# Weight segments in every second group of inputs, and the bias of q as a 129th column of the correlation

## What is computed

```python
q = layernorm(x) @ Wq + bq;  k = ctx @ Wq + bq;  v = k      # 16 columns each
corr = real(ifft(fft(q) * conj(fft(k)))).mean(batch, head)   # along the 128 positions
W, I = top_k(corr, 12);  W = softmax(W)
R = sum_j W[j] * roll(v, -I[j])
x = x + repeat(R) @ Wout + bout
x = x + fp4_linear(silu(fp4_linear(n, w_gate)) * fp4_linear(n, w_up), w_down)   # n = layernorm(x)
```

## Time and profile before

| | |
|---|---|
| Median of 3 runs | 572.26 us (572.17 to 574.67) |
| The profiled execution | 570.98 us, of which the span is 569.2 us |
| PE busy | 466.8 us (82%), 3454 instructions |
| DVE busy | 463.4 us (81%), 748 |
| ACT busy | 394.4 us (69%), 666 |
| POOL busy | 284.1 us (50%), 366 |
| DMA | 69.19 MB moved, mean 122 GB/s |

### The profile page before, as it was taken

The page is one execution under the profiler, slowest core; times in us unless marked ns, Lnnn a source line. Parts: engine busy times, 40 slices in busy tenths (PEclk is TensorE's granted clock), DMA queues, the critical chain, the costliest instruction groups (busy, mean ns, idle before and its releaser), DMA issues. The chain is left out here.

```text
span 569.2 us, 10045 instructions
## 1 busy us (share of the span) xinstructions
PE 466.8 (82%) x3454; PEld 307.0 (54%) x3454; DVE 463.4 (81%) x748; ACT 394.4 (69%) x666; POOL 284.1 (50%) x366
## 2 busy tenths in 40 slices
PE   5277995408799899998989999998999999999944
PEld 5266994303355555655556555565555655556633
DVE  2899657356889999989999999998999999997760
ACT  2378555456887778888887777888888777776530
POOL 3053530066556665565566666555556666622231
PEclk9699998757899999999999999999999999999977
DMA  9965930323246665555655576555655556445433
GB/s 276 306 220 157 293 119 15 87 57 76 51 84 119 128 118 113 107 123 120 124 117 106 126 117 129 108 109 129 120 117 116 112 126 109 95 89 107 79 78 78
DMA packets 165042, 69.19 MB, mean 122 GB/s; under 512 B 129152, under 2 KB 164736, under 8 KB 164992
## 3 DMA queue, kind: packets, MB, share of 16 engines
q1 hardware_dynamic: 164416, 68.03, 52.9%
q10 hardware_dynamic: 576, 0.53, 0.3%
HBM read 27.90 MB, written 9.18 MB: 65 GB/s over the span
## 5 line engine op out<-in xcount | busy, mean ns | idle before, releaser
L723 PE MATMUL ps<-guT_hi,a_xT 128*128 128x512 f16 (+1 forms) x384 | 140.6, 366 | 50.3 <-DMA a_xT<-ctx_sb 50.3
L428 POOL TENSOR_TENSOR ctx_sb<-h_c,sl 128x704 f16<-128x704 f16 x64 | 96.1, 1523 | 115.8 <-DVE ctx_sb L953 115.8
L733 PE MATMUL ps<-dT_hi,hqT 128*128 128x256 f16 x704 | 132.5, 277 | 11.9 <-DMA hqT<-ctx_sb 11.9
L724 PE MATMUL ps<-guT_lo,a_xT 128*128 128x512 f16 (+1 forms) x384 | 140.3, 365 | 0.0
L725 PE MATMUL ps<-guT_hi,a_xT 128*128 128x512 f16 (+1 forms) x384 | 140.0, 365 | 0.0
L723 PEld LDWEIGHTS ps<-guT_hi,a_xT 128*128 128x128 f16 x384 | 37.8, 98 | 98.6 <-DMA a_xT<-ctx_sb 40.4
L735 PE MATMUL ps<-dT_lo,hqT 128*128 128x256 f16 x384 | 89.6, 277 | 0.0
L482 ACT ACTIVATE h_c<-y_h 128x1408 bf16<-128x1408 bf16 (+3 forms) x40 | 49.2, 1230 | 55.2 <-DVE y_h L983 35.0
L733 PEld LDWEIGHTS ps<-dT_hi,hqT 128*128 128x128 f16 x704 | 70.0, 99 | 25.0 <-DMA hqT<-ctx_sb 12.7
L466 POOL TENSOR_TENSOR xs<-xs,w_raw 128x512 f32<-128x512 f32 x32 | 38.1, 1192 | 69.5 <-issue 49.1
L948 DVE SCALAR_TENSOR_TENSOR hb<-ps,h_in,w_raw 128x704 f32<-128x704 f32 x64 | 60.5, 945 | 2.6 <-PE ps L725 2.5
(11 more groups left out here) (140 smaller groups left out, 854.9 us busy)
## 6 DMA issues: line engine op xcount, KB each, us to landing
w_raw<-a_scratch SPq DMA_DIRECT2D x64, 128.5 KB, 2.7
xs<-in_x_dram SPq DMA_DIRECT2D x16, 512.0 KB, 5.7
ctx_sb<-in_ctx_dram SPq DMA_DIRECT2D x16, 512.0 KB, 4.5
out_dram<-a_xT SPq DMA_DIRECT2D x64, 128.0 KB, 2.0
hqT<-ctx_sb SPq DMA_TRANSPOSE x64, 3.7
w_raw<-in_L_ffn_w_down_dram SPq DMA_DIRECT2D x1, 704.0 KB, 5.2
w_raw<-in_L_ffn_w_gate_dram SPq DMA_DIRECT2D x1, 640.0 KB, 5.9
w_raw<-in_L_ffn_w_up_dram SPq DMA_DIRECT2D x1, 640.0 KB, 7.1
```

The lines of the kernel that those rows point to most:

```text
L428: pool.tensor_tensor(hq[:, j % 2, t, FF:2 * FF].rearrange("p (ih r) -> p ih r", ih=IH), h_c[:, :].bitcast(F16).rearrange("p (ih t r) -> p ...
L723: pe.matmul(dst, xt[:, c, :], guT[0][:, c, n0:n1], start=(c == 0), stop=False)
L724: pe.matmul(dst, xt[:, c, :], guT[1][:, c, n0:n1], start=False, stop=False)
L733: pe.matmul(dst, hqT[:, j % 4, c, :], dT_hi[:, c, :], start=(c == 0), stop=False)
```

## The change

The segments of w_gate and w_up are spread: a function `turn(i)` gives the segment whose turn comes in group `i`. With `W_FIRST = 0` segments 0 to 5 are begun in groups 0, 2, 4, 6, 8 and 10. `w_split` goes with `turn(i)`, `w_finish` with `turn(i - 1)`, `w_hi` and `w_lo` with `turn(i - 2)`; the order of the calls inside a group stays.

The product of k with bq is no longer issued. q and k of a group, which lay in one tile, lie in two; the one for q has a 129th column that holds bq and is written once, before the loop. The product of k and q takes 129 columns, and bank 7 holds the sum of the bias in its column 128. After the loop ScalarE takes this column into `g_bias` and adds it, as a bias per partition, in both copies of `g2`, in the function Identity where it was Copy.

```diff
--- before.py
+++ after.py
@@ -54,6 +54,7 @@
 SEGS = [(256 * c, 256 * min(2, GU_CH - c)) for c in range(0, GU_CH, 2)] + [(256 * GU_CH + FF * j, FF) for j in range(2)]
 WCOLS = 256 * GU_CH + 2 * FF
 N_GU = len(SEGS) - 2
+W_FIRST = 0
 NP = B // 2
 IH = BLK // 2
 RUN_H, RUN_X = 2 * NBH, 2 * NBX
@@ -133,9 +134,11 @@
         ident_out = sb("ident_out", [P, P])
         wq_x = sb("wq_x", [P, KC, SLOT])
         a_xT = sb("a_xT", [P, 2, 2 * QT, P])
-        qkT = sb("qkT", [P, 2, 2, P])
+        qT = sb("qT", [P, 2, P + 1])
+        kT = sb("kT", [P, 2, P])
         v_all = sb("v_all", [P, B * DH])
         g2 = sb("g2", [P, 2, P])
+        g_bias = sb("g_bias", [P, 1])
         dg = sb("dg", [P, P])
         corr = sb("corr", [P, 3, P + 4])
         top = sb("top", [P, 2, 8])
@@ -194,7 +197,7 @@
             "c_loaded0", "c_loaded1", "c_loaded2", "c_loaded3", "attn_loaded0", "attn_loaded1",
             "stored0", "stored1", "stored2", "stored3", "consts", "w_steps", "w_pool", "w_lo", "w_hi", "w_split", "root_set", "w_tr", "w_ev",
             "stats", "pool_a", "wq_sum", "r_ev", "wq_mid", "trx", "trc", "evx", "evc", "proj", "qk_ev", "v_tr", "v_ev",
-            "g_done", "g_ev", "g_io", "t_steps", "t_pe", "t_exp", "t_io", "a_io0", "a_io1", "a_io2", "a_io3", "m_sums",
+            "q_bias", "g_done", "g_col", "g_ev", "g_io", "t_steps", "t_pe", "t_exp", "t_io", "a_io0", "a_io1", "a_io2", "a_io3", "m_sums",
             "x1_done", "sq_done", "pool_st", "xn_ready", "x_max", "sc_steps", "sh_done", "s32", "sl", "x_split", "x4_steps",
             "h_steps", "h_split", "h4_steps", "loh", "o_done", "id_out",
             "hT0", "hT1", "hT2", "hT3", "xT0", "xT1", "gate_done", "gu_done", "sil_done", "d_done")}
@@ -227,6 +230,10 @@
         def scratch(w, g):
             o, n = SEGS[g]
             return w[:, FF * max(0, g - N_GU):FF * max(0, g - N_GU) + n]
+
+        def turn(i):
+            k = i - W_FIRST
+            return k // 2 if k >= 0 and k % 2 == 0 and k // 2 < N_GU else None
 
         def seg_at(g):
             return 7 + K_W * g + (7 if g >= N_GU else 0)
@@ -414,8 +421,8 @@
             for i in range(NQ):
                 if i + 2 < NQ:
                     rstd_a(i + 2)
-                if 0 <= i - 2 < N_GU:
-                    w_lo(i - 2)
+                if turn(i - 2) is not None:
+                    w_lo(turn(i - 2))
 
             largest(1)
 
@@ -515,13 +522,15 @@
                     evac_x(i, u)
                 if i % QT == 2 and i > QT:
                     keep_v(i // QT - 1)
-                if 0 <= i < N_GU:
-                    w_split(i)
-                if 0 <= i - 2 < N_GU:
-                    w_hi(i - 2)
+                if turn(i) is not None:
+                    w_split(turn(i))
+                if turn(i - 2) is not None:
+                    w_hi(turn(i - 2))
             act.wait_ge(s["g_done"], NQ)
-            act.activation(g2[:, 0, :], bank(7)[:, 0:P], ACT.Copy).then_inc(s["g_ev"], 1)
-            act.activation(g2[:, 1, :], bank(7)[:, 0:P], ACT.Copy).then_inc(s["g_ev"], 1)
+            act.activation(g_bias[:, :], bank(7)[:, P:P + 1], ACT.Copy).then_inc(s["g_col"], 1)
+            act.wait_ge(s["g_col"], 1)
+            for k in range(2):
+                act.activation(g2[:, k, :], bank(7)[:, 0:P], ACT.Identity, bias=g_bias[:, 0:1]).then_inc(s["g_ev"], 1)
 
             keep_v(NQ // QT - 1)
             evacuate_weights(act, range(EARLY))
@@ -633,11 +642,12 @@
 
             def correlate(i):
                 pe.wait_ge(s["qk_ev"], i + 1)
-                pe.matmul(bank(7)[:, 0:P], qkT[:, i % 2, 1, :], qkT[:, i % 2, 0, :], start=(i == 0), stop=False)
-                pe.matmul(bank(7)[:, 0:P], qkT[:, i % 2, 1, :], bq_col[:, :].broadcast_to([P, P]), start=False, stop=(i == NQ - 1)
+                if i == 0:
+                    pe.wait_ge(s["q_bias"], 1)
+                pe.matmul(bank(7)[:, 0:P + 1], kT[:, i % 2, :], qT[:, i % 2, :], start=(i == 0), stop=(i == NQ - 1)
                           ).then_inc(s["g_done"], 1)
                 need(pe, s["v_ev"], i // QT)
-                pe.transpose(bank(6)[:, P * (i % QT):P * (i % QT + 1)], qkT[:, i % 2, 1, :], ident[:, :]).then_inc(s["v_tr"], 1)
+                pe.transpose(bank(6)[:, P * (i % QT):P * (i % QT + 1)], kT[:, i % 2, :], ident[:, :]).then_inc(s["v_tr"], 1)
 
             for i in range(NQ):
                 for u in range(2):
@@ -823,10 +833,10 @@
                 need(dve, s["g_done"], i - 1)
                 need(dve, s["v_tr"], i - 1)
                 out = bank(4 + i % 2)
-                dve.tensor_scalar(qkT[:, i % 2, 1, :], out[:, P:2 * P], bq_col[:, 0:1], None, ALU.add)
-                dve.tensor_copy(qkT[:, i % 2, 0, :], out[:, 2 * P:3 * P]).then_inc(s["r_ev"], 1)
+                dve.tensor_scalar(kT[:, i % 2, :], out[:, P:2 * P], bq_col[:, 0:1], None, ALU.add)
+                dve.tensor_copy(qT[:, i % 2, 0:P], out[:, 2 * P:3 * P]).then_inc(s["r_ev"], 1)
                 dve.wait_ge(s["r_ev"], i + 1)
-                dve.tensor_tensor(qkT[:, i % 2, 0, :], out[:, 0:P], qkT[:, i % 2, 0, :], ALU.mult).then_inc(s["qk_ev"], 1)
+                dve.tensor_tensor(qT[:, i % 2, 0:P], out[:, 0:P], qT[:, i % 2, 0:P], ALU.mult).then_inc(s["qk_ev"], 1)
 
             def w_prepare(part):
                 cols = cols_of(part * N_GU)[0]
@@ -859,18 +869,21 @@
                 last = dve.scalar_tensor_tensor(out=wq_x[:, c, :], in0=bank(7)[:, 0:SLOT], scalar=-1.0 / D, in1=wq_sb[:, c, :],
                                                 op0=ALU.mult, op1=ALU.add)
             last.then_inc(s["wq_mid"], 1)
+            for k in range(2):
+                last = dve.tensor_copy(qT[:, k, P:P + 1], bq_col[:, :])
+            last.then_inc(s["q_bias"], 1)
             w_prepare(0)
             for i in range(NQ):
                 if i + 2 < NQ:
                     stats_a(i + 2)
                 if i >= 1:
                     evac_qk(i - 1)
-                if i == 0:
+                if i == W_FIRST:
                     w_scales(0)
-                if 0 <= i - 1 < N_GU:
-                    w_finish(i - 1)
-                if 0 <= i < N_GU:
-                    w_segment(i)
+                if turn(i - 1) is not None:
+                    w_finish(turn(i - 1))
+                if turn(i) is not None:
+                    w_segment(turn(i))
             evac_qk(NQ - 1)
             cs = s["c_steps"]
 
```

## The result

The changed kernel took 565.99 us (median of 4 runs, 564.98 to 567.59) against 572.24 (4 runs, 572.17 to 574.67) for the kernel before in the same job: ratio 0.989, 95% interval 0.9861 to 0.9918. That is 6.25 us less; the forecast was 7.0 less and 565.3. The profiled execution is the slowest of the four, 567.59 us, of which 565.8 is span.

What follows compares the result with a forecast made beforehand. VectorE's queue bounds the first part at 5.44 us a group, TensorE the second at 3.72. Summed chains bring p(15), the last project's end, from 88.75 to 81.78, 7.0 earlier: 572.26 - 7.0 = 565.3 us, range 562.0 to 568.9.

Steps and rivals of the forecast that it cites:

- The pace of the pairs: Correlation stage: during the segments two groups take 7.7 to 8.1 us, TensorE waiting for ScalarE before every second group's transposes.
- p(next odd) = E + 7.57: Chain over ScalarE: from E, evac_qk's start on VectorE, to p, project's end in the next odd group, 7.57 us.
- the last segment: End of the segments: it has half the columns, estimated at 0.9 us less in the chain over ScalarE.
- E(1): Start of VectorE's evac_qk in group 1: stays at 30.76 us, since GpSimd returns from its all-reduce only at 27.43.
- The meetings: VectorE's w_finish beside GpSimd's w_lo in each pair: w_finish takes 2.36 us, without a meeting 1.51.
- The power of rstd: Rival: GpSimd's pow blocks VectorE's w_finish, 3.14 us in two or three pairs; 566.9 us, chance 0.10.
- TensorE alone: Rival: ScalarE's late evacuations never reach TensorE, all groups take 3.50 us; 560.2 us, chance 0.10.
- the gain is not there: Rival: something else sets the first part's 5.44 us a group, only the removed product pays; 570.5 us, chance 0.05.
- the clock falls: Rival: stalls moved to every second group make TensorE's clock fall in the stage; slower, chance 0.05.
- Behind it the same times: After the correlation's hand-over: unedited code keeps its times; wrong if its length changes by more than 1 us.
- The table load of the upper end: ScalarE's Identity with bias at the copies of g: a table load, over 1 us, not expected, only in the upper bound.
- The product's 0.23 per group: TensorE in the correlation stage: without the second product an unhindered group falls from 3.72 to 3.49, say 3.50 us.

Runs made afterwards that it cites:

- e1: The changed kernel run again in another job, nothing edited: 565.56 us, ratio 0.9883 to the kernel before.
- e2: Against the kernel before: the segments spread over every second group, the separate product of k with bq kept; 565.37 us, ratio 0.9877.
- e6: Against e2: two unused tiles of 4 bytes a partition that move g2 alone by 32 bytes; 565.57 us, ratio 0.989.
- e9: Against the changed kernel: 16 matmuls with overwritten results at the head of TensorE's queue, putting back the 64 removed instructions; 565.06 us, ratio 0.989.
- e4: Against the changed kernel: GpSimd's w_lo one group later, so that it meets no w_finish; 565.13 us, ratio 0.9875.
- e5: Against the changed kernel: g_bias declared ahead of kT, so that g2 begins at a multiple of 64 bytes; 566.53 us, ratio 0.9903.
- e10: Against e2: two more one-column copies on VectorE into an unused tile before w_prepare(0); 565.71 us, ratio 0.9889.
- e3: Against the changed kernel: the segments in groups 0 to 5 as before, the 129th column kept; 572.44 us, ratio 1.0003.

## Why the prediction was right, and what it had wrong

**The pace of the pairs was right, and so was its mechanism.** The sum said p(next odd) = E + 7.57. In the trace after, E is 31.19, 39.56, 47.50, 55.80, 63.51 and the next odd p lies 7.60, 7.57, 7.56, 7.57 and 7.00 behind; the last segment, half as long, was put at 6.67. The stage came to 51.74 where the working gives 81.78 - 29.43 = 52.35. The first pair took 7.75, not 8.90. I had E(1) at 30.76 = p(1) + 1.33, as if GpSimd always came back from its all-reduce at 27.43; over the thirteen traces it comes back between 26.31 and 27.43, and p(1) moves as well. In e1, e2, e6 and e9 p(3) lies 10.89 or 10.90 behind GpSimd's return, which is the prediction's own distance (38.33 - 27.43); in after, e4, e5 and e10, where TensorE is the later one, 7.73 to 7.75 behind p(1). So the chain was right, and the 1.15 us that the first pair gave on top of it is an accident of where these two lie in one execution, not an effect of the change. Against that, p(3) to p(11) took 31.72 where I had 31.20, and p(11) to p(15) 12.27 for 12.25: -1.15 + 0.52 + 0.02 is the -0.61 between 51.74 and 52.35. The last segment is most of the 0.52: its chain was 7.00 and not 6.67.

**The meetings were right in kind.** They fall on L816 (my L769 or L806 of the old numbering) in three of five segments. That VectorE can win, and w_lo wait, was not in the sum. The trace after shows both directions: where w_lo began first (36.20 against 36.38), it kept its 1.17 and L816 took 1.53 instead of 0.69; where L816 began first (60.57 against 60.58), it kept its 0.69 and w_lo took 1.70. The power of rstd did not hold VectorE: L775 ran inside it at 0.41, and L779 began inside it and took 0.42. That rival has fallen, as the earlier trace rows had it.

**TensorE alone** fell with the waits of 0.46 and 1.05 for ScalarE; **the gain is not there** with e2; **the clock falls** with 0.95 and 1.00 in the first stage. The clock did fall elsewhere: in the feed-forward block, and in the stage of e3.

**"Behind it the same times" was wrong.** That step said that what follows p(15) moves as one piece. It grew from 480.45 (569.2 - 88.75) to 482.46 in e1 and 483.02 in the trace after, beyond the 1 us that I had named as the bound. Its pieces in the trace after: 0.16 ahead of the write, which I had put at nothing (g_bias costs 0.20 and the missing product gives back 0.21, but the two copies with a bias take 0.65 us from the first one's start to the write's issue, where the two without took 0.48, and I had them at the same price); 0.75 in the write; 0.28 in the read; 0.39 in other small parts up to the gates, with the diagonals' products at 0.80 instead of 0.49 us; 0.99 in the feed-forward block. The table load of the upper end did not come: ScalarE's two in the trace after, 1.28 us each as in the trace before, are ahead of the first evacuation and at L542 (L533 before), none is at the copies. The step had failed in its premise: unedited code is not unaffected code. Three instruction streams (TensorE's, VectorE's, ScalarE's) had changed their count. For the write (e9) and the gap (e10) that is shown; for the fallen clock, the longer read and the small parts it is not.

**The product's 0.23 per group was right where it stands, and no gain of it can be seen in the end.** It makes the stage 1.5 to 2.1 us shorter. e3 shows no gain (1.0003, with its clock disturbed), e1 none over e2. That the total came out only 0.7 above the forecast, although 2.0 to 2.6 us are lost behind the stage, is in good part luck: the stage gave 7.6 (59.32 - 51.74) and not 6.97, the first pair's accident among it, and the rest lies within the scatter of single executions. Summed from e1: 59.32 - 51.73 = 7.59, less 2.01 behind and 0.18 of p(1), is 5.40, the difference of the spans; with the traced execution of before 1.2 below its median (572.15), 6.6.

What stays open: p(1) varies from 29.25 to 31.04 over the profiles of kernels that split segment 0 in group 0 (29.61 and 31.04 in the changed kernel itself), and no run tells what sets it. And why the granted clock differs at L724, and between executions of one kernel.

## What to carry to other kernels

Read the span in stretches, find the queue whose chain closes the loop of a pair of steps (here VectorE to ScalarE to TensorE), and sum that chain from starts, not from busy times: it gave 7.57 to within 0.03 in four pairs. Spread work that need not be done at once over the steps, so that no queue has a step longer than TensorE's; that was worth 6.8 us, and moving the split out of the first evacuations' way 2.8 to 3.2 more. A cut on an engine that has just become the bound must be measured to the end of the program: 1.5 us of the stage was saved here, the traces show it lost again behind the stage, and none of it can be seen in the medians.

## What the runs showed that I had not expected

- The DMA view lists a queue "instruction" beside those of the data (q8: 27 packets, 0.44 MB, in the trace after). With one such packet 0.06 to 0.19 us ahead, a write of 128 KB took 1.93 to 2.53 us instead of 1.71 to 1.76, and ended 1.16 to 1.21 us after that packet each time. 64 more instructions on TensorE, whose results nobody uses, moved the packet away (e9).
- Two more instructions in VectorE's queue brought a gap of 0.36 us at one fixed instruction of pair 11, some 270 us later (e10). In the traces of six of the ten kernels that have the gap TensorE's granted clock falls to 0.50 behind it, which takes 1.0 us more; whether the gap brings that is not shown.
- A power of 128x4 numbers on GpSimd, 1.01 us long, did not hold VectorE at all (L775 at 0.41 and L779 at 0.42 beside it), while a product of 128x512, 1.17 us long, did (L816 at 1.53 instead of 0.69). Whether it is the size or the operation was not tried.
- GpSimd's return from one all-reduce varies from 26.31 to 27.43 us over the traces, and where it is the later one it moves p(3) one for one.
